# Forming the remainder of each context chunk on GpSimd instead of VectorE, in a gated cross-attention block

## The reference

```python
xn = layernorm(x)
q = xn @ Wq.T + bq;  k = ctx @ Wk.T + bk;  v = ctx @ Wv.T + bv      # 16 heads of 16
p = softmax(mask(clip(q k^T / 4, -50, 50)))                          # over the 1444 context tokens
delta = layernorm(rs * ((p v) @ Wo.T + bo)) * gamma + beta
x1 = x + tanh(g_xattn) * delta
h = quant(layernorm(x1)); h = silu(h @ w1q) * (h @ w2q)              # 704 wide, ternary weights
out = x1 + tanh(g_ffn) * (quant(h) @ w3q)
```

## Time and profile before

| | before |
|---|---|
| median of 3 runs | 1439.22 us |
| the profiled execution, its own time | 1438.62 us |
| its span, first to last instruction | 1436.8 us |
| PE busy | 1348.5 us, 94% |
| DVE busy | 1131.2 us, 79% |
| ACT busy | 965.1 us, 67% |
| POOL busy | 469.7 us, 33% |
| mean granted TensorE clock | 0.974 |

### The profile page before, as it was taken

The page is one execution under the profiler, slowest core; times in us unless marked ns, Lnnn a source line. Parts: engine busy times, 40 slices in busy tenths (PEclk is TensorE's granted clock), DMA queues, the critical chain, the costliest instruction groups (busy, mean ns, idle before and its releaser), DMA issues.

```text
span 1436.8 us, 48034 instructions
## 1 busy us (share of the span) xinstructions
PE 1348.5 (94%) x19984; PEld 1220.3 (85%) x19984; DVE 1131.2 (79%) x2241; ACT 965.1 (67%) x1634; POOL 469.7 (33%) x759
## 2 busy tenths in 40 slices
PE   5699999999999999999999999999999999999982
PEld 5599888888988888898888898888889888888971
DVE  6668788878878887877887887888788788878763
ACT  2367776676776767777676777767777767676751
POOL 3523333233333223233323333332333332232310
PEclk9699999999999999999999999999999999999995
DMA  7467666666766666776667676666667666766620
GB/s 217 110 160 174 157 153 156 164 158 167 169 163 155 154 163 166 168 169 156 156 152 171 161 176 160 158 150 161 163 162 173 158 157 155 167 163 162 139 52 8
DMA packets 142477, 222.13 MB, mean 155 GB/s; under 512 B 29162, under 2 KB 135598, under 8 KB 142254
## 3 DMA queue, kind: packets, MB, share of 16 engines
q1 hardware_dynamic: 129966, 199.31, 57.7%
q0 software_dynamic: 12288, 19.69, 6.2%
HBM read 54.00 MB, written 3.28 MB: 40 GB/s over the span
## 4 chain that ended last, share of the span: by engine, by line
PE 52%; DVE 25%; ACT 13%; issue 7%; POOL 2%; SPq 1%; DMA 0%; DVEq 0%; POOLq 0%; ACTq 0%
PE pvb L1212 13%; PE sc L1192 12%; PE cb L1233 11%; PE cb L1247 9%; ACT e_sb L549 7%; DVE e_sb L783 4%; DVE zt L855 3%; DVE c_lo L750 2%; PE mb L1280 2%; PE mb L1271 2%; DVE tiny L935 2%; PE mb L1298 2%; DVE k_lo L774 2%; DVE th L945 1%; ACT us L623 1%
## 5 line engine op out<-in xcount | busy, mean ns | idle before, releaser
L549 ACT ACTIVATE e_sb<-sc 121x800 f32<-121x800 f32 (+1 forms) x768 | 644.8, 844 | 201.4 <-PE sc L1192 191.3
L1192 PE MATMUL sc<-q_st,k_st 96*121 96x200 f32 (+1 forms) x3072 | 476.4, 278 | 7.1 <-DMA q_st<-bd_hi 3.1
L1192 PEld LDWEIGHTS sc<-q_st,k_st 96*121 96x121 f32 (+1 forms) x3072 | 416.3, 186 | 42.5 <-issue 9.0
L783 DVE TENSOR_SCALAR e_sb<-e_sb,hi_b 121x1600 f32<-121x1600 f32 (+1 forms) x384 | 399.4, 1047 | 38.3 <-ACT e_sb L549 38.1
L1212 PE MATMUL pvb<-e_sb,v_sb 121*32 121x100 f32 x12288 | 286.2, 251 | 0.1
L1212 PEld LDWEIGHTS pvb<-e_sb,v_sb 121*32 121x32 f32 x12288 | 264.7, 110 | 22.6 <-issue 19.0
L774 DVE SCALAR_TENSOR_TENSOR k_lo<-cb,bk_c,k_hi 128x484 fp32r<-128x484 f32 (+1 forms) x192 | 134.4, 700 | 137.8 <-ACT k_hi L561 137.8
L1247 PE MATMUL cb<-wv_hi,c_hi 128*121 128x256 f32 (+1 forms) x768 | 227.8, 297 | 15.2 <-DVE k_lo L774 12.2
L475 POOL DMA_DIRECT2D q_st<-bd_hi x256 | 183.2, 719 | 107.9 <-DVE bd_lo L829 104.7
L1247 PE MATMUL cb<-wv_hi,c_lo 128*121 128x256 f32 (+1 forms) x768 | 217.0, 283 | 0.0
L1247 PE MATMUL cb<-wv_lo,c_hi 128*121 128x256 f32 (+1 forms) x768 | 216.9, 282 | 0.0
(11 more groups left out here) (139 smaller groups left out, 1609.0 us busy)
## 6 DMA issues: line engine op xcount, KB each, us to landing
k_st<-k_hi SPq DMA_DIRECT2D x512, 121.0 KB, 2.8
c_in<-in_ctxT SPq DMA_DIRECT2D x64, 484.0 KB, 3.8
k_st<-k_lo SPq DMA_DIRECT2D x256, 121.0 KB, 2.9
k_st<-k_hi SPq DMA_DIRECT2D x256, 119.0 KB, 2.3
c_in<-in_ctxT SPq DMA_DIRECT2D x32, 476.0 KB, 3.6
k_st<-k_lo SPq DMA_DIRECT2D x128, 119.0 KB, 2.4
q_st<-bd_hi POOLq DMA_DIRECT2D x256, 50.0 KB, 3.3
q_st<-bd_lo POOLq DMA_DIRECT2D x128, 50.0 KB, 3.2
```

Source lines behind the costliest of these rows:

```text
L549: nc.scalar.activation(e_sb[e_slot(b, n)][0:TL[n], k * SW:(k + 1) * SW].rearrange("p (o c) -> p o c", o=2), sc[q % NSC][0:TL[n], :, 0:2 * PW],
L783: V.tensor_scalar(e, e, E_LO, hi_b[b.par][0:TL[n], n:n + 1], ALU.max, ALU.min).then_inc(clip_done, 1)
L1192: last = T_.matmul(sc[q % NSC][0:TL[n], e // 2, (e % 2) * PW:(e % 2 + 1) * PW], k_st[st_slot(b, n // TPC)][:, pr // NQ, pr % NQ, t0:t0 + T ...
```

## The change

`c_lo` of a chunk is no longer formed by DVE in `batch` but by POOL, in a new function `chunk_rest`, which waits for the cast. The one semaphore `split_done`, which counted casts and remainders together, becomes two, `c_hi_done` and `c_lo_done`; PE and SP wait for the second. POOL runs `chunk_rest` at the head of its steps n = 2, 5 and 9, for chunks 0, 1 and 2 of the next sequence. The first sequence's three remainders, in the setup, stay on DVE.

```diff
                 if nxt:
-                    sp.wait_ge(split_done, SPLIT.after(b.plus(1), "lo0"))
+                    sp.wait_ge(c_lo_done, CHUNK.after(b.plus(1), 0))
                     load_c(b.plus(1), 2)
...
+            def chunk_rest(b, u):
+                slot, _n = c_slot(b, u)
+                w = CL[u]
+                pool.wait_ge(c_hi_done, CHUNK.after(b, u))
+                alone()
+                nc.gpsimd.tensor_tensor(c_lo[slot][:, :, 0:w], c_in[slot][:, :, 0:w],
+                                        c_hi[slot][:, :, 0:w].bitcast(f32), ALU.subtract).then_inc(c_lo_done, 1)
+
...
             def batch(b, nxt, prev):
                 for n in range(NT):
+                    if nxt and n in (2, 5, 9):
+                        chunk_rest(b.plus(1), n // 4)
                     if n == 3:
...
-                V.tensor_copy(c_hi[slot][:, :, 0:w], c_in[slot][:, :, 0:w]).then_inc(split_done, 1)
+                V.tensor_copy(c_hi[slot][:, :, 0:w], c_in[slot][:, :, 0:w]).then_inc(c_hi_done, 1)
...
                     if nxt and n == 6:
                         q_rest(c)
-                    if nxt and n % 4 == 1:
-                        split_rest(c, n // 4)
...
                     if o == 0:
-                        pe.wait_ge(split_done, SPLIT.after(b, f"lo{u}"))
+                        pe.wait_ge(c_lo_done, CHUNK.after(b, u))
```

More of the change, by code:

```diff
@@ L208, in flamingo_block @@
         pe_ctx, pe_x, pe_post = sem("pe_ctx"), sem("pe_x"), sem("pe_post")
-        split_done, k_lo_done = sem("split_done"), sem("k_lo_done")
+        c_hi_done, c_lo_done, k_lo_done = sem("c_hi_done"), sem("c_lo_done"), sem("k_lo_done")
         k_hi_done, v_done, act_post = sem("k_hi_done"), sem("v_done"), sem("act_post")
@@ L215, in flamingo_block @@
         CLEAN = ("gt", "lt", "pos", "nan", "put_gt", "put_lt")
-        SPLIT = Steps(*(f"{p}{u}" for u in range(NCH) for p in ("hi", "lo")))
+        CHUNK = Steps(*range(NCH))
         CTX = Steps(*(f"{w}{u}{i}" for u in range(NCH) for w in ("k", "v") for i in range(2)))
@@ L353, in batch @@
                 if nxt2:
-                    sp.wait_ge(split_done, SPLIT.after(b.plus(1), "lo1"))
+                    sp.wait_ge(c_lo_done, CHUNK.after(b.plus(1), 1))
                     load_c(b.plus(2), 0)
@@ L358, in batch @@
                 if nxt2:
-                    sp.wait_ge(split_done, SPLIT.after(b.plus(1), "lo2"))
+                    sp.wait_ge(c_lo_done, CHUNK.after(b.plus(1), 2))
                     load_c(b.plus(2), 1)
@@ L367, in passes @@
                 load_x(whole(1, base))
-                sp.wait_ge(split_done, SPLIT.after(whole(0, base), "lo0"))
+                sp.wait_ge(c_lo_done, CHUNK.after(whole(0, base), 0))
                 load_c(whole(0, base), 2)
                 stack_k(whole(0, base), 0)
-                sp.wait_ge(split_done, SPLIT.after(whole(0, base), "lo1"))
+                sp.wait_ge(c_lo_done, CHUNK.after(whole(0, base), 1))
                 load_c(whole(1, base), 0)
                 stack_k(whole(0, base), 1)
-                sp.wait_ge(split_done, SPLIT.after(whole(0, base), "lo2"))
+                sp.wait_ge(c_lo_done, CHUNK.after(whole(0, base), 2))
                 load_c(whole(1, base), 1)
@@ L748, in split_rest @@
                 w = CL[u]
-                dve.wait_ge(split_done, SPLIT.after(b, f"hi{u}"))
+                dve.wait_ge(c_hi_done, CHUNK.after(b, u))
                 V.tensor_tensor(c_lo[slot][:, :, 0:w], c_in[slot][:, :, 0:w], c_hi[slot][:, :, 0:w].bitcast(f32),
-                                ALU.subtract).then_inc(split_done, 1)
+                                ALU.subtract).then_inc(c_lo_done, 1)
             def watched(b, i, rows_=P):
```

## The result

The changed kernel took 1503.49 us (median of 4 runs, 1502.44 to 1503.93), the kernel before beside it on the same chip 1439.41 us (4 runs, 1439.09 to 1439.96). The ratio is 1.0444, with a 95% interval of 1.0426 to 1.0462. That is 64 us more, where 39.3 were forecast. The time lies inside the outer range of 1446 to 1512 us and outside the 1468 to 1490 that the forecast gave itself; the nearest value on record is the rival's 1506.

A forecast was written before the change was run, and what follows sets the result against it. PE, busy 94% of the span, was taken as the bound, with DVE's chain to delta setting the period. 0.66 + 0.08 + 0.57 = 1.31 us times 30 gives 39.3, so 1479 us; range 1468 to 1490, outer 1446 to 1512.

The forecast's parts named there:

- the rival's 1506: POOL gets in wherever it asked first, ahead of x1_norm at chunk 1: +1.02 there, 2.25 a period, 1506 us; chance 0.18.
- The mechanism and the sign: POOL and DVE exclude each other a whole instruction at a time on certain SBUF operations; slower, chance 0.80.
- Chunk 0: At n = 1 POOL's c_lo goes ahead of the clip and holds it, delaying delta: +0.66 us a period.
- POOL's duration: A 968-column subtraction on POOL takes 2.19 us, by a line through x_res and wv_lo.
- Chunk 1: At n = 5 the clip runs first, x1_norm follows, then POOL gets in and slightly delays L916: +0.08 us a period.
- The second half of the step: At n = 5 x1_norm follows the clip at once and keeps POOL out until 620.41.
- Chunk 2: At n = 9 and 10 POOL's c_lo and x_res run back to back and hold th: +0.57 us a period.
- lower bound: Chunk 2 costs 0 if th gets in between c_lo and x_res: its +0.71 fits inside DVE's idle time.
- The idle 0.73: DVE's idle time in us at 638.77, waiting for the last exponential, which can absorb delay from chunk 2.
- The wait on PE: PE's wait at delta grows to 2.0 us from 0.77, and the one at L1247 becomes 0.3.
- A misreading without effect: SP's waits sit ahead of loads used a batch later, so moving the remainders costs nothing there.
- The count of 30: The move happens in 31 batches; the first has no attention behind it to delay, so 30 periods pay.

The follow-up runs named there:

- the kernel with its own wait: Against the kernel before, only chunk 1's subtraction moved to POOL, where it waits for POOL's own second root of the period: 1465.55 us, ratio 1.0186.

## Why the prediction was right in sign and short in size

- **The mechanism and the sign held.** The three remainders lie under two-input or clip instructions of DVE that are held until POOL is through, and each one made the period longer.
- **Chunk 0: right.** Forecast 0.66 with a clip of 2.79; measured 0.62 and 2.74, and 42.83 - 42.21 = 0.62 alone.
- **POOL's duration: right.** Estimated 2.19 from a smaller subtraction, measured 2.26.
- **Chunk 1: this step failed.** Forecast 0.08, measured 1.12 alone. From c_hi to k_lo behind x2q it takes 5.15 us before and 6.28 after (643.41 to 649.69). The forecast took the clip of the earlier trace rows as being in before c_lo can ask; the runs show the clip held until c_lo is through, 3.26 us instead of 1.05. Why it was not in is argued, not shown: it may have been waiting for d_rstd. Held clips end 0.85 us after POOL's instruction does (chunk 0: c_lo to 673.68, the clip to 674.53), and the one of before ended at 620.09, 0.87 after d_rstd at 619.22, so that such a wait would be too short to show in its duration. In the changed kernel c_lo, queued right behind d_rstd, goes on ahead of the clip. The row that shows this stood in the forecast's own evidence: wv_lo at 10.53 follows x_rstd without a gap while DVE's c_lo from 10.24 waits, 2.58 us. The second half of the step, that DVE going straight on keeps POOL out, is refuted for c_lo by the kernel with its own wait, though x_res, at n = 10 of the changed kernel, was kept out by th and then the clip. The rival of 1506 us has the size of this (+1.02), but named x1_norm as the one held, which only that kernel shows. That the outer range holds the measured time is therefore luck: it reaches that far to cover this rival, whose instruction is not the one that the changed kernel shows held.
- **Chunk 2: mis-sized downward.** Forecast 0.57, measured 0.31. The forecast let x_res follow c_lo at once and hold th over both. In usual periods th got in between the two, which the working had as its lower bound, and lost 0.62 us; x_res then held gs for another 0.52, which that bound lacked. The idle 0.73 before the clip was used up first.
- **The wait on PE: expected in the wrong place.** It was expected to grow in front of the delta matmuls, from 0.77 to 2.0. It stayed at 0.75, and the two in front of the value matmuls grew to 1.17 and 1.08, since DVE's k_lo stands ahead of y_out and PE reaches its matmul first.
- **Terms that the forecast lacked.** POOL's pause, three times, which turned th from 1.14 into 2.79: 3.4 us. And the clock: no time in the changed kernel, but about 10 us where chunk 0 goes alone.
- **A misreading without effect.** Not all of SP's loads are used a batch later: the one behind c_lo of chunk 0 brings chunk 2, which DVE casts at n = 9 of the same batch. That cast (653.99 in the changed kernel) follows the clip before it without idle time.
- **The count of 30 held** to within one (29 periods, and most of one more at the end), so the sum 0.66 + 0.08 + 0.57 is to be read against 0.62 + 1.13 + 0.31: chunk 1 alone makes up for more than the whole difference of 0.75 a period.

## What to carry to other kernels

Before work moves from VectorE to GpSimd, put the two timelines over each other and ask which VectorE instruction is in flight for as long as the moved one takes; that, and not GpSimd's idle share, is the price. The move of chunk 0 costs 2.2% ahead of a clip and gains 2.1% beneath PSUM read-outs, a shuffle and a reciprocal; one wait makes the difference. Where a short GpSimd instruction has a long one queued right behind it, count with both.

## What the runs showed of the hardware that was not expected

- A clip that started at 644.63, inside a d_rstd ending at 644.81, was passed by a c_lo that followed it back to back; with 0.17 us between the two, and c_lo 0.2 us later, it got in. But it is no rule that the follower wins: behind c_lo, th passed x_res in the usual periods (1.14), and x_res passed th where th had waited since 484.10 (2.79). Nor does the earlier start decide it: c_lo with a lead of 0.37 us over the clip won, x_res with 0.38 lost to it, and d_ve and dn, with the same starts, came out both ways. What gives the turn at such a change stays open.
- With chunk 0 alone on POOL, PE's granted clock stood at 0.51 behind two waits of 0.76 us with 1.0 us of work between them, and 8 periods of 30 were 1.3 us longer for it. Why only those, and why none behind the longer waits of the changed kernel's usual periods (1.08 and 0.75), stays open.
- POOL pauses for 0.94 to 1.25 us every ten periods among its DMA issues, in each of these kernels. Where the order on DVE rests on how far POOL is ahead, this is enough to change who waits.
